# Grouped-query attention, 32 heads: the turns of the step three back are issued ahead of the new scores in each step, instead of behind them

## The chip, the core and the metric

One core of a Trainium2 chip. The metric is the device time of one execution, in microseconds; lower is better. The program has five instruction streams: TensorE (PE; its weight loads are shown as PEld), VectorE (DVE), ScalarE (ACT), GpSimd (POOL) and the DMA queues that SyncE and GpSimd feed. They meet only at semaphores.

## The reference

A chain of four cross-attention layers on `x` (2, 512, 512) against a context (2, 1024, 512). The change lies in the second, layer L1:

```python
H, NH, KVH, HD = 512, 32, 8, 16        # 32 heads of 16, 8 key/value heads
q = hidden_state @ Wq + bq             # 512 rows
k = encoder_hidden_state @ Wk + bk     # 1024 rows
v = encoder_hidden_state @ Wv + bv
q = q.reshape(b, l, KVH, GROUPS, HD).transpose(0, 2, 3, 1, 4)
...
scores = jnp.einsum('bkgld,bksd->bkgls', q, k) * scale
scores = scores + encoder_attention_mask[:, :, None, :, :]
attn = jax.nn.softmax(scores, axis=-1)
out = jnp.einsum('bkgls,bksd->bkgld', attn, v)
out = out.transpose(0, 3, 1, 2, 4).reshape(b, l, H)
out = out @ Wo + bo
x = out + hidden_state                 # then a layer norm
```

The other layers (one-head attention, 16 heads of 128 twice with an MLP, 16 heads of 32 with an MLP) are the same in both kernels.

## The kernel before

The program runs a list of stages for batch 0 and then again for batch 1. The stage of layer L1 is the function `grouped`. Its main loop has 128 steps and a tail of 16 (`STEPS`, `TAIL`): four groups c of eight heads (one quarter of the 512 columns), and in a group 8 heads x 4 blocks of 128 query rows. A step q is one head and one block: 128 rows against 1024 keys. It goes through the engines as a pipeline:

- S(q), TensorE, line 767 (777 after): the scores, two products of 48 x 128 by 48 x 512 into two PSUM banks. There are two pairs of banks, used in turn. S(q) waits for `s_free`: D(q-2) has read this pair.
- D(q), VectorE, line 904: adds the mask, negates, takes the row's minimum, and writes the result to `units` in SBUF (a ring of U = 5). It signals `s_free`.
- E(q), ScalarE, line 850: the exponential in place, with the row sum. It is issued one step later (`LAG_E` = 1) and signals `e_done`.
- T(k), TensorE, line 779 (757 after): eight transposes of 128 x 128 that turn the probabilities, in two halves h of four, each into a bank of its own. They are issued in step q = k + 3 (`LAG_T` = 3). Each half waits for `e_done` of step k and for `t_free[h]`: the copy of the half of T(k-1) has been made. There is a single bank for each half.
- The copies out of these banks, in the same step: the first half by ScalarE (line 858), the second by VectorE (line 915, C(k) below), right behind D(q) on VectorE. Each signals its `t_free`.
- PV, TensorE, line 791: for each head two groups of four products with the values, issued in steps 8 and 9 behind the head's first (`LAG_PV` = 8), so two steps in four have one.

One ring bank serves the rest, behind PV in the steps of `ring_in`: the query projection of the next group (three products in each of steps 16 to 19 of a group), the spread of the reciprocals (step 4), the fold of the parts (step 7: line 813 on TensorE, then lines 928 and 930 on VectorE with line 875 of ScalarE between them), and the output projection (three products in each of steps 10 to 13, added by VectorE, line 936).

Each engine takes its instructions in the order in which its function issues them: `pe_`, `act_` and `dve_` all loop over the same q. In `act_` a step is E(q-1), then the copy of the first half of T(q-3). In `dve_` a step is D(q), then C(q-3):

```python
dve.wait_ge(s_full, n + 1)
dve.tensor_tensor_reduce(units[...], ps[...], mask[...], ...).then_inc(s_free, 1)
...
k = q - LAG_T
dve.wait_ge(t_full[1], n + 1)
dve.tensor_copy(turned[...], ps[:, T_BANK + 1, :]...).then_inc(t_free[1], 1)
```

Of the kernel before, what the change touches and what calls it, by code (L numbers as in the profile page):

```python
# [30 lines left out]
P = 128  # L31
# [77 lines left out]
def build(nc, t, out):  # L109
# [3 lines left out]
    def sem(name):  # L113

        if name not in sems:
            sems[name] = ctx.enter_context(nc.semaphore(name))
        return sems[name]

    with ctx:
        uid = [0]  # L120

        def sb(stack, name, shape, dt=F32):
            uid[0] += 1
            return stack.enter_context(nc.sbuf_tensor(f"{name}_{uid[0]}", shape, dt))
# [29 lines left out]
        ps = ctx.enter_context(nc.psum_tensor("ps", [P, 8, 512], F32))  # L154
        S_BANK, T_BANK, R_BANK = 0, 4, 6


        ident = sb(ctx, "ident", [P, P])
# [376 lines left out]
        def grouped():  # L535
# [4 lines left out]
            U = 5  # L540
            STEPS = C * 32
            TAIL = 16
            LAG_E, LAG_T, LAG_PV = 1, 3, 8
# [5 lines left out]
            units = sb(own, tag + "_units", [P, U, NK])  # L549
# [30 lines left out]
            e_done = sem(tag + "_exp_done")  # L580
            t_full = [sem(f"{tag}_turn_full{i}") for i in range(2)]
            t_free = [sem(f"{tag}_turn_free{i}") for i in range(2)]
# [8 lines left out]
            def ring_of(x):  # L591
                return ps[:, x[2], :] if x[0] == "o" and x[1] == C - 1 else ring
# [14 lines left out]
            def upto(eng, s, n):  # L607
                if n > 0:
                    eng.wait_ge(s, n)

            def ring_turn(pe, b, x):
                if x[0] == "o" and x[1] == C - 1:
                    pe.wait_ge(s_free, (b + 1) * STEPS)
                elif ring_at[x]:
                    y, n = ring_jobs[ring_at[x] - 1], b * 2 * C
                    s_, n = {"q": (kq_done, b * KQ + 2), "rzb": (rzb_done, n), "fold": (a32_done, n),
                             "o": (o_added, n * LT)}[y[0]]
                    pe.wait_ge(s_, n + 1 + (y[1] * LT + y[2] if y[0] == "o" else y[1]))
# [106 lines left out]
            def pe_kv(pe, b, n, w):  # L725
                pe.wait_ge(split["kv"], b * 2 + n + 1)
                for h in range(2):
                    for k in range(KC):
                        i = mm3(pe, ps[:, 2 * n + h, :], w[:, k, :], CT[:, k, h * 512:(h + 1) * 512],
                                k == 0, k == KC - 1)  # L730
                    i.then_inc(pre_full, 1)

            def pe_(pe, b):
                pe_kv(pe, b, 0, wk)
                pe.wait_ge(split["q"], b * C + 1)
                ring_turn(pe, b, ("q", 0))
                pe_q(pe, b, 0, range(KC))
                pe_kv(pe, b, 1, wv)
                for h in range(2):
                    pe.wait_ge(v_done, b * 4 + h + 1)  # L740
                    for q in range(4):
                        i = pe.transpose(ps[:, T_BANK + h, q * P:(q + 1) * P],
                                         vt[:, (4 * h + q) * P:(4 * h + q + 1) * P], ident[:, :])
                    i.then_inc(pre_full, 1)
                pe.wait_ge(kq_done, b * KQ + 2)
                pe.wait_ge(v_done, b * 4 + 4)
                pe.wait_ge(made, b + 1)
                for q in range(STEPS + TAIL):
                    c = q // 32
                    if q < STEPS:  # L750
                        n, i_, u = b * STEPS + q, q % 4, q % 32 // 4
                        if q == 0:
                            pe.wait_ge(first_ready, (b + 1) * 2 * 6 * 16)
                        elif q == 4:
                            pe.wait_ge(qs_ready[0], (b * 15 + 3) * 6 * 16)
                        elif q % 32 == 0:
                            pe.wait_ge(qs_ready[0], (b * 15 + 3 + 4 * c) * 6 * 16)
                        elif q % 32 == 16:
                            pe.wait_ge(qs_ready[1], (b * C + c + 1) * 4 * 6 * 16)
                        if q == 16:  # L760
                            pe.wait_ge(ks_ready[0], (b + 1) * 6 * 16)
                        elif q == 32:
                            pe.wait_ge(ks_ready[1], (b + 1) * 6 * 6 * 16)
                        upto(pe, s_free, n - 1)
                        for h in range(2):
                            p0 = 64 * h
                            i = pe.matmul(ps[:, 2 * (q % 2) + h, :],  # L767
                                          qs[p0:p0 + 3 * DH, u, i_ * P:(i_ + 1) * P],
                                          ks[p0:p0 + 3 * DH, 2 * c + u // 4, :],
                                          start=True, stop=True, skip_group_check=True)  # L770
                        i.then_inc(s_full, 1)
                    k = q - LAG_T
                    if 0 <= k < STEPS:
                        n = b * STEPS + k
                        pe.wait_ge(e_done, n + 1)
                        for h in range(2):
                            upto(pe, t_free[h], n)
                            for v in range(4):
                                i = pe.transpose(ps[:, T_BANK + h, v * P:(v + 1) * P],  # L779
                                                 units[:, k % U, (4 * h + v) * P:(4 * h + v + 1) * P], ident[:, :])  # L780
                            i.then_inc(t_full[h], 1)
                    hd, h = divmod(q - LAG_PV, 4)
                    if 0 <= hd < C * HEADS and h < 2:
                        pair = b * (C * 4) + hd // 2
                        pe.wait_ge(t_free[h], b * STEPS + 4 * hd + 4)
                        if hd % 2 == 0 and h == 0:
                            upto(pe, o_free, pair)
                        for j in range(4):
                            v, kv = 4 * h + j, hd // 4
                            lhs = vd[:, v, kv, 16:48] if hd % 2 == 0 else vd[:, v, kv, 0:32]  # L790
                            i = pe.matmul(ps[32 * j:32 * j + 32, O_BANK, :], lhs, turned[:, hd % 2, v, :],
                                          start=hd % 2 == 0 and h == 0, stop=hd % 2 == 1 and h == 1,
                                          skip_group_check=True)
                        i.then_inc(pv_done, 1)
                    if q % 32 in (16, 17, 18) and c + 1 < C:
                        if q % 32 == 16:
                            pe.wait_ge(split["q"], b * C + c + 2)
                            ring_turn(pe, b, ("q", c + 1))
                        pe_q(pe, b, c + 1, (q % 32 - 16,))
                    for x in ring_in[q]:  # L800
                        if x[0] == "q":
                            pe_q(pe, b, c, (3,))
                            continue
                        g = b * C + x[1]
                        ring_turn(pe, b, x)
                        if x[0] == "rzb":
                            pe.wait_ge(rzx_done, g + 1)
                            for lt in range(LT):
                                i = pe.transpose(ring[:, lt * P:(lt + 1) * P], rzx[:, lt, :], ident[:, :])
                        elif x[0] == "fold":  # L810
                            pe.wait_ge(o_free, (g + 1) * 4)
                            for p_ in range(4):
                                i = pe.matmul(ring[32 * p_:32 * p_ + 32, :], fold[:, :], parts[:, p_, :],
                                              start=True, stop=True, skip_group_check=True)
                        else:
                            lt = x[2]
                            if lt == 0:
                                pe.wait_ge(att_done, b * 2 * C + x[1] + 1)
                                pe.wait_ge(split["o"], g + 1)
                            i = mm3(pe, ring_of(x), att[:, lt * P:(lt + 1) * P], wo[:, :], True, True)  # L820
                        i.then_inc(ring_full, 1)
                barrier(pe, done, b)
# [1420 lines left out]
```

## Time and profile before

| | |
|---|---|
| median of three runs | 4287.23 us (4285.82 to 4290.34) |
| the profiled execution | 4284.18 us, its span 4282.4 us |
| instructions in the span | 55226 |
| PE busy | 3984.2 us, 93% of the span |
| DVE busy | 2556.9 us, 60% |
| ACT busy | 1868.4 us, 44% |
| granted TensorE clock, mean | 0.974 |

The rows further down come from this one profiled execution, which lies 3.05 us under the median. Times are microseconds from the start of the span. The loop of the grouped stage runs from about 153 to 451 us for batch 0 and from about 2291 to 2590 us for batch 1. The two levels of the granted clock are 1.00 (2.4 GHz) and 0.50 (1.2 GHz).

### The profile page before, as it was taken

To read this page: it belongs to the slowest core of one execution; us is meant where nothing else is said; L and a number is where in the kernel's file an instruction comes from. 1 tells how busy PE (TensorE), PEld (TensorE's weight loads), DVE (VectorE), ACT (ScalarE), POOL (GpSimd) and SP (SyncE) were. 2 spreads that over 40 slices of the span, in tenths; PEclk is the share of its full clock that TensorE was granted. 3 is DMA by queue.
4 is the path that set the end of the run, shared out by engine and by line. 5 is a ranking of instruction groups with operands and counts; after the bars stand their busy time and mean duration, and the time that the engine had idled before them with its cause. 6 is when DMAs were issued, how large, how long until landed. Compare 5 with 4: busy or idle time off the path is not lost. (4 is left out here: it accounts for less than half of the span.)

```text
span 4282.4 us, 55226 instructions
## 1 busy us (share of the span) xinstructions
PE 3984.2 (93%) x21018; PEld 2967.9 (69%) x21018; DVE 2556.9 (60%) x4134; ACT 1868.4 (44%) x3294; POOL 1189.7 (28%) x1318
## 2 busy tenths in 40 slices
PE   8899799998999989999988998999989999899988
PEld 6555588887888867543775556888878888775437
DVE  3588656556565665455636886565565656645555
ACT  3588434344443431455135884344343434314551
POOL 0642213223231323121306422132232313232213
PEclk9999899999999999999999999999999999999999
DMA  2310101011010113221403101010110101132212
GB/s 70 74 31 18 55 23 45 23 45 40 28 40 28 40 40 90 51 52 30 130 30 77 28 18 55 23 45 29 39 40 28 45 23 40 45 89 50 50 35 87
DMA packets 167573, 195.62 MB, mean 46 GB/s; under 512 B 18627, under 2 KB 123272, under 8 KB 167310
## 3 DMA queue, kind: packets, MB, share of 16 engines
q1 hardware_dynamic: 142734, 151.15, 11.6%
q0 software_dynamic: 24576, 40.94, 5.0%
q8 instruction: 169, 2.77, 0.3%
q14 instruction: 94, 0.77, 0.1%
HBM read 149.02 MB, written 2.10 MB: 35 GB/s over the span
## 5 line engine op out<-in xcount | busy, mean ns | idle before, releaser
L1337 DVE TENSOR_TENSOR w_pt_lo<-ps,w_pt_hi 128x512 fp32r<-128x512 f32 x512 | 334.7, 685 | 158.7 <-ACT w_pt_hi L1268 158.6
L1113 POOL CAST w_wo_hi<-w_raw 128x1024 fp32r<-128x1024 f32 x32 | 33.2, 1037 | 1329.7 <-PE ps L149 1324.0
L1268 ACT ACTIVATE w_pt_hi<-ps 128x512 fp32r<-128x512 f32 x512 | 281.3, 595 | 203.7 <-PE ps L1205 203.6
L904 DVE CUSTOM_DVE_ANT_0 g_units<-ps,g_mask 128x1024 f32<-128x1024 f32 x256 | 311.2, 1217 | 81.2 <-PE ps L767 81.2
L1754 ACT ACTIVATE h_pt<-ps,zero_col 128x512 f32<-128x512 f32 x384 | 257.1, 686 | 234.3 <-PE ps L1710 232.8
L1803 DVE TENSOR_REDUCE h_mxs<-ps 128x1 f32<-128x512 f32 x384 | 243.7, 684 | 162.5 <-PE ps L1699 160.8
L1320 DVE TENSOR_REDUCE w_mx<-ps 128x1 f32<-128x1024 f32 x256 | 312.0, 1219 | 33.8 <-PE ps L149 33.3
L1205 PE MATMUL ps<-ident,w_p 128*128 128x128 f32 x2048 | 279.1, 275 | 39.6 <-DVE w_pt_lo L1337 39.6
L779 PE MATMUL ps<-ident,g_units 128*128 128x128 f32 x2048 | 292.2, 284 | 19.7 <-ACT g_turned L858 17.4
L850 ACT ACTIVATE g_units<-g_units,g_nmx 128x1024 f32<-128x1024 f32 x256 | 294.6, 1151 | 18.8 <-DVE g_nmx L904 15.8
L1205 PEld LDWEIGHTS ps<-ident,w_p 128*128 128x128 f32 x2048 | 235.2, 140 | 96.2 <-DVE w_pt_lo L1337 67.1
L147 PE MATMUL ps<-w_wv_hi,CT_hi 128*128 128x256 f32 x1024 | 289.1, 282 | 8.6 <-DVE w_v_lo L1331 8.6
L779 PEld LDWEIGHTS ps<-ident,g_units 128*128 128x128 f32 x2048 | 222.0, 143 | 100.1 <-issue 64.3
L149 PE MATMUL ps<-w_wv_hi,CT_lo 128*128 128x256 f32 x1024 | 288.5, 282 | 0.0
L148 PE MATMUL ps<-w_wv_lo,CT_hi 128*128 128x256 f32 x1024 | 288.4, 282 | 0.0
L1261 ACT ACTIVATE w_p<-ps,w_nm 128x1024 f32<-128x1024 f32 x256 | 281.1, 1098 | 0.0
L1259 ACT ACTIVATE w_ex<-w_xl,w_nm 128x1 f32<-128x1 f32 x256 | 75.5, 295 | 420.7 <-DVE w_nm L1326 420.7
L1296 DVE SCALAR_TENSOR_TENSOR w_k_lo<-ps,cols,w_k_hi 128x512 fp32r<-128x512 f32 x128 | 95.7, 750 | 212.0 <-ACT w_k_hi L1243 212.0
L147 PE MATMUL ps<-w_pt_hi,w_v_hi 128*128 128x512 f32 x512 | 217.3, 424 | 0.0
L147 PE MATMUL ps<-w_k_hi,w_q_hi 128*128 128x512 f32 x512 | 210.3, 411 | 7.1 <-ACT w_p L1261 7.1
L1681 PE MATMUL ps<-h_pt,h_vd 128*64 128x512 f32 x768 | 210.5, 626 | 6.6 <-ACT h_parts L1762 6.0
L147 PEld LDWEIGHTS ps<-w_wv_hi,CT_hi 128*128 128x128 f32 x1024 | 195.9, 191 | 14.7 <-DVE w_v_lo L1331 9.4
(362 smaller groups left out, 10209.2 us busy)
## 6 DMA issues: line engine op xcount, KB each, us to landing
w_raw<-in_L_xattn_wk SPq DMA_DIRECT2D x32, 512.0 KB, 3.4
w_raw<-in_L_xattn_wq SPq DMA_DIRECT2D x32, 512.0 KB, 3.5
w_raw<-in_L_xattn_wv SPq DMA_DIRECT2D x32, 512.0 KB, 3.8
w_raw<-in_L_xattn_wo SPq DMA_DIRECT2D x32, 512.0 KB, 3.6
mlp_raw<-in_L_xattn_w_fc SPq DMA_DIRECT2D x64, 256.0 KB, 3.2
mlp_raw<-in_L_xattn_mlp_w SPq DMA_DIRECT2D x64, 256.0 KB, 3.2
h_ks<-h_k_hi POOLq DMA_DIRECT2D x64, 192.0 KB, 3.0
g_qs<-g_q_hi POOLq DMA_DIRECT2D x256, 32.0 KB, 1.9
```

What stands on the lines that cost most here:

```text
L147: pe.matmul(o, a[0], b[0], start=start, stop=False, skip_group_check=True)
L148: pe.matmul(o, a[0], b[1], start=False, stop=False, skip_group_check=True)
L149: return pe.matmul(o, a[1], b[0], start=False, stop=stop, skip_group_check=True)
L779: i = pe.transpose(ps[:, T_BANK + h, v * P:(v + 1) * P], units[:, k % U, (4 * h + v) * P:(4 * h + v + 1) * P], ident[:, :])
L850: act.activation(units[:, k % U, :], units[:, k % U, :], ACT.Exp, bias=nmx[:, k % U:k % U + 1], scale=-1.0, accum_out=z[:, k // 32 % 2, lt ...
L904: dve.tensor_tensor_reduce(units[:, q % U, :].rearrange("p (h w) -> p h w", h=2), ps[:, 2 * (q % 2):2 * (q % 2) + 2, :], mask[:, q % 4, :] ...
L1205: i = pe.transpose(ps[:, T_BANK + tn % 2, lt * P:(lt + 1) * P], prob[:, u, lt, v * P:(v + 1) * P], ident[:, :])
L1261: act.activation(prob[:, u, lt, :].rearrange("p (h w) -> p h w", h=2), ps[:, S_BANK + 2 * (sn % 2):S_BANK + 2 * (sn % 2) + 2, :], ACT.Exp, ...
L1268: act.activation(pt.h[:, x[2] % 4, :], ps[:, T_BANK + tn % 2, :], ACT.Copy).then_inc(t_hi, 1)
L1320: dve.tensor_reduce(mx[:, u, lt:lt + 1], ps[:, S_BANK + 2 * (sn % 2):S_BANK + 2 * (sn % 2) + 2, :], AX.XY, ALU.max).then_inc(max_own, 1)
L1337: dve.tensor_tensor(pt.l[:, x[2] % 4, :], ps[:, T_BANK + tn % 2, :], as_f32(pt.h[:, x[2] % 4, :]), ALU.subtract).then_inc(t_free, 1)
L1754: act.activation(pt[:, j, :], ps[:, T_BANK_ + (m * KT + j) % 2, :], ACT.Exp, bias=zero_col[:, :], scale=SCALE).then_inc(e_done, 1)
```

## The change

In `pe_` the block that issues T(q-3) moves from behind S(q) to ahead of it. Nothing else changes: no operation is added or removed, the semaphores and their counts are the same, and the streams of the other engines are the same.

```diff
                 for q in range(STEPS + TAIL):
                     c = q // 32
+                    k = q - LAG_T
+                    if 0 <= k < STEPS:
+                        n = b * STEPS + k
+                        pe.wait_ge(e_done, n + 1)
+                        for h in range(2):
+                            upto(pe, t_free[h], n)
+                            for v in range(4):
+                                i = pe.transpose(ps[:, T_BANK + h, v * P:(v + 1) * P],
+                                                 units[:, k % U, (4 * h + v) * P:(4 * h + v + 1) * P], ident[:, :])
+                            i.then_inc(t_full[h], 1)
                     if q < STEPS:
                         n, i_, u = b * STEPS + q, q % 4, q % 32 // 4
...
                         i.then_inc(s_full, 1)
-                    k = q - LAG_T
-                    if 0 <= k < STEPS:
-                        n = b * STEPS + k
-                        pe.wait_ge(e_done, n + 1)
-                        for h in range(2):
-                            upto(pe, t_free[h], n)
-                            for v in range(4):
-                                i = pe.transpose(ps[:, T_BANK + h, v * P:(v + 1) * P],
-                                                 units[:, k % U, (4 * h + v) * P:(4 * h + v + 1) * P], ident[:, :])
-                            i.then_inc(t_full[h], 1)
                     hd, h = divmod(q - LAG_PV, 4)
```

TensorE's instructions in the plain steps 9 and 10 of the first batch, before (L767 is S, L779 T, L791 PV; `g_scores_free` is `s_free`, `g_exp_done` is `e_done`, `g_turn_free1` is `t_free[1]`):

```order
L767 MATMUL ps<-g_ks,g_qs 128x512 [waits g_scores_free]
L767 MATMUL ps<-g_ks,g_qs 128x512
L779 MATMUL ps<-ident,g_units 128x128 [waits g_turn_free0,g_exp_done]
L779 MATMUL ps<-ident,g_units 128x128 x3
L779 MATMUL ps<-ident,g_units 128x128 [waits g_turn_free1]
L779 MATMUL ps<-ident,g_units 128x128 x3
L791 MATMUL ps<-g_turned,g_vd 32x512 [waits g_turn_free1]
L791 MATMUL ps<-g_turned,g_vd 32x512 x3
L767 MATMUL ps<-g_ks,g_qs 128x512 [waits g_scores_free]
```

The same place after (L777 is S, L757 T):

```order
L777 MATMUL ps<-g_ks,g_qs 128x512 [waits g_scores_free]
L777 MATMUL ps<-g_ks,g_qs 128x512
L791 MATMUL ps<-g_turned,g_vd 32x512 [waits g_turn_free1]
L791 MATMUL ps<-g_turned,g_vd 32x512 x3
L757 MATMUL ps<-ident,g_units 128x128 [waits g_turn_free0,g_exp_done]
L757 MATMUL ps<-ident,g_units 128x128 x3
L757 MATMUL ps<-ident,g_units 128x128 [waits g_turn_free1]
L757 MATMUL ps<-ident,g_units 128x128 x3
L777 MATMUL ps<-g_ks,g_qs 128x512 [waits g_scores_free]
```

PV now follows S at once, and between PV and the next S stand the eight turns with their two waits.

The second place is the step of the fold (step 7 of the second head group), on TensorE before; L813 is the fold:

```order
L779 MATMUL ps<-ident,g_units 128x128 [waits g_turn_free1]
L779 MATMUL ps<-ident,g_units 128x128 x3
L813 MATMUL ps<-g_parts,g_fold 32x512 [waits g_o_free,rzb_done]
L813 MATMUL ps<-g_parts,g_fold 32x512 x3
L767 MATMUL ps<-g_ks,g_qs 128x512 [waits g_scores_free]
```

and after:

```order
L777 MATMUL ps<-g_ks,g_qs 128x512 [waits g_scores_free]
L777 MATMUL ps<-g_ks,g_qs 128x512
L813 MATMUL ps<-g_parts,g_fold 32x512 [waits g_o_free,rzb_done]
L813 MATMUL ps<-g_parts,g_fold 32x512 x3
L757 MATMUL ps<-ident,g_units 128x128 [waits g_turn_free0,g_exp_done]
L757 MATMUL ps<-ident,g_units 128x128 x3
L757 MATMUL ps<-ident,g_units 128x128 [waits g_turn_free1]
```

The fold now stands right behind the scores of its step. VectorE's stream, which is the same in both kernels, has at this place the copy, the two operations that follow the fold, and the next pass over scores:

```order
L904 ISA g_units,g_nmx<-ps,g_mask 128x1024 [waits g_turn_full1,g_scores_full]
L904 ISA g_nmx 128x1
L915 COPY g_turned<-ps 128x4x128 [waits g_turn_full1,g_pv_done]
L928 TENSOR_TENSOR g_a_61<-ps,g_rzb 128x512 [waits rzb_done,g_ring_full]
L930 SCALAR_TENSOR_TENSOR g_att_lo<-g_a_61,cols,g_att_hi 128x512 [waits att_hi]
L904 ISA g_units,g_nmx<-ps,g_mask 128x1024 [waits g_turn_full1,g_scores_full]
```

Nothing moved there; what moved is when TensorE hands it the scores of the last row.

## Rows read from the trace of the kernel before

**Rows 1.** The page: span, and busy time by engine.

```profile
span 4282.4 us, 55226 instructions
...
PE 3984.2 (93%) x21018; PEld 2967.9 (69%) x21018; DVE 2556.9 (60%) x4134; ACT 1868.4 (44%) x3294; POOL 1189.7 (28%) x1318
```

**Rows 2.** Windows: the first batch's loop, S(0) to past S(127); clock after the engines.

```profile
core 0: us, PE busy (x) PEld busy (x) DVE busy (x) ACT busy (x) POOL busy (x), PEclk, DMA share, GB/s
153.30:443.40 290.10, 276.02 (x1844) 154.53 (x1844) 240.97 (x405) 232.34 (x403) 128.53 (x245) 0.98 0.17 31
```

**Rows 3.** Waits in the first batch's loop: total, times, longest.

```profile
DVE g_units L904 <- PE ps L767: 40.7, 53, 3.2
...
PE ps L779 <- ACT g_turned L858: 7.8, 24, 0.5
...
PEld ps L779 <- DVE g_turned L915: 3.3, 10, 0.4
```

**Rows 4.** Order of time, TensorE only, plain steps: start, duration, instruction.

```profile
431.74 0.50 PE L767 MATMUL ps<-g_ks,g_qs 48*128 48x512 f32 x2
432.17 1.09 PE L779 MATMUL ps<-ident,g_units 128*128 128x128 f32 x8
433.19 0.49 PE L767 MATMUL ps<-g_ks,g_qs 48*128 48x512 f32 x2
...
436.50 1.06 PE L791 MATMUL ps<-g_turned,g_vd 128*32 128x512 f32 x8
437.50 0.51 PE L767 MATMUL ps<-g_ks,g_qs 48*128 48x512 f32 x2
...
439.95 0.50 PE L767 MATMUL ps<-g_ks,g_qs 48*128 48x512 f32 x2
```

**Rows 5.** Order of time, VectorE in the first of these steps.

```profile
432.28 1.22 DVE L904 CUSTOM_DVE_ANT_0 g_units<-ps,g_mask 128x1024 f32<-128x1024 f32 x1 [0.61 <-PE ps L767]
...
433.43 0.69 DVE L915 COPY g_turned<-ps 128x512 f32<-128x512 f32 x1
```

**Rows 6.** Order of time: a second half that waited for VectorE's copy.

```profile
332.91 1.21 DVE L904 CUSTOM_DVE_ANT_0 g_units<-ps,g_mask 128x1024 f32<-128x1024 f32 x1
...
334.05 0.69 DVE L915 COPY g_turned<-ps 128x512 f32<-128x512 f32 x1
...
334.78 0.42 PEld L779 LDWEIGHTS ps<-ident,g_units 128*128 128x128 f32 x4 [0.29 <-DVE g_turned L915]
335.37 0.18 PEld L767 LDWEIGHTS ps<-g_ks,g_qs 48*128 48x128 f32 x2 [0.17 <-issue]
```

**Rows 7.** Order of time, TensorE: S to S with PV and three projection products.

```profile
339.10 0.50 PE L767 MATMUL ps<-g_ks,g_qs 48*128 48x512 f32 x2
...
342.45 0.50 PE L767 MATMUL ps<-g_ks,g_qs 48*128 48x512 f32 x2
```

**Rows 8.** Order of time, VectorE: the first operation behind the fold, the next pass.

```profile
315.60 0.69 DVE L928 TENSOR_TENSOR g_a<-ps,g_rzb 128x512 f32<-128x512 f32 x1
...
317.75 1.22 DVE L904 CUSTOM_DVE_ANT_0 g_units<-ps,g_mask 128x1024 f32<-128x1024 f32 x1
```

**Rows 9.** Order of time: steps 4 and 5 of batch 0, clock at 0.50.

```profile
162.05 0.80 PE L767 MATMUL ps<-g_ks,g_qs 48*128 48x512 f32 x2 [3.12 <-DMA g_qs<-g_q_lo]
...
162.77 1.97 PE L779 MATMUL ps<-ident,g_units 128*128 128x128 f32 x8
162.88 1.23 DVE L904 CUSTOM_DVE_ANT_0 g_units<-ps,g_mask 128x1024 f32<-128x1024 f32 x1 [3.23 <-PE ps L767]
...
164.67 0.79 PE L767 MATMUL ps<-g_ks,g_qs 48*128 48x512 f32 x2
```

**Rows 10.** Order of time, TensorE: S(127) of batch 0, S(4) and S(127) of batch 1.

```profile
441.40 0.49 PE L767 MATMUL ps<-g_ks,g_qs 48*128 48x512 f32 x2
...
2299.38 0.79 PE L767 MATMUL ps<-g_ks,g_qs 48*128 48x512 f32 x2 [2.92 <-DMA g_qs<-g_q_lo]
...
2580.10 0.49 PE L767 MATMUL ps<-g_ks,g_qs 48*128 48x512 f32 x2
```

**Rows 11.** Windows: a stretch of the next stage, and the loop's first 11.7 us.

```profile
504.00:508.00 4.00, 2.32 (x10) 1.61 (x9) 1.83 (x4) 3.34 (x7) 0.00 (x0) 1.00 0.51 140
...
153.30:165.00 11.70, 6.84 (x28) 4.44 (x28) 6.81 (x12) 6.21 (x11) 11.70 (x25) 0.61 0.49 70
```

## The prediction

> **What bounds the kernel now.** Read the page first for which engine is full, then the windows to find out whether that holds in the stage that the change touches, then the waits, and last the order of time, because only there is it seen who releases whom. The page has TensorE busy for 93% of a span of 4282.4 us [rows 1]. The grouped stage runs twice, once a batch, and its main loop is 128 steps long; over that loop TensorE is busy for 276.0 of 290.1 us at a granted clock of 0.98, VectorE for 241.0 and ScalarE for 232.3 [rows 2]. So TensorE bounds the loop, but VectorE is close behind: per step 290.1 / 128 = 2.27 us, of which VectorE works 1.88. The waits are small on TensorE's side: the turns wait 7.8 us in all for the copies of ScalarE, their weight loads 3.3 us for those of VectorE, while VectorE waits 40.7 us for scores [rows 3]. That last wait is no loss: VectorE is the faster of the two and runs out of scores in the steps in which TensorE also has a weighted sum to do.
>
> In what follows S(q) is the score product of step q, D(q) VectorE's pass over it (line 904), T(k) the eight turns of step k, in two halves, C(k) VectorE's copy of the second half (line 915), and PV the four products of a weighted sum. In the order of time a step without PV takes TensorE 433.19 - 431.74 = 1.45 us, of which S to T is 0.43 and T to the next S 1.02; a step with PV takes 439.95 - 437.50 = 2.45, the PV being 437.50 - 436.50 = 1.00 [rows 4]. Two steps in four have one.
>
> **Why the order matters.** T(q-3)'s second half needs the bank that C(q-4) empties. VectorE does C(q-4) right behind D(q-1), and D(q-1) needs S(q-1). Before, S(q) stands ahead of T(q-3), so while VectorE is busy with D(q-1) and C(q-4) the next scores are already being made, and D(q) follows C(q-4) without a pause. After, S(q) stands behind T(q-3) and so behind its wait. TensorE can't make S(q) until C(q-4) has ended, and VectorE, whose next instruction is D(q), stands still meanwhile. What was a chain over two steps with a score bank in hand becomes a ring through both engines in each step. That S could slip past is excluded by the trace: at 334.78 the second half of a turn starts 0.04 us after the end of the copy that held it, and the scores behind it start at 335.37, although the D of two steps back, all that they wait for, had ended by 332.91 + 1.21 = 334.12; TensorE ran them in order [rows 6].
>
> **The price of the ring, link by link.** From S's start to D's start 432.28 - 431.74 = 0.54 us [rows 4, 5]. D to C 433.43 - 432.28 = 1.15, C itself 0.69 [rows 5]. From the end of C (334.05 + 0.69 = 334.74) to the second half's weight load 0.04; from there to the S behind it 335.37 - 334.78 = 0.59 [rows 6]. The sum is 3.01 us a step. Nothing else of a plain step is longer: TensorE needs 1.45 or 2.45, ScalarE 232.3 / 128 = 1.82 [rows 2]. PV and the first half of T lie beside D and C, at no cost, since 2.45 is under 3.01; were that cover gone, a step would cost its 2.45 and more. ScalarE's exponential and its copy gain slack.
>
> *Steps.* The first four steps of a batch fill the pipe and step 4 waits for a DMA until 162.05 in any case [rows 9]; from there to S(127) are 123 steps, 441.40 - 162.05 = 279.35 us in the first batch and 2580.10 - 2299.38 = 280.72 in the second [rows 9, 10]: 560.1 in both. After: 246 x 3.01 = 740.5.
>
> *Steps in which TensorE is longer than the ring.* A PV step that also holds three products of the next projection or of the output projection takes 342.45 - 339.10 = 3.35 us of TensorE [rows 7], 0.34 over the ring. By the code these are steps 12 and 13 of three head groups and 16 and 17 of three: 12 a batch, 24 x 0.34 = 8.2. The same products in steps without PV (3.35 - 1.00 = 2.35) are covered now.
>
> *The fold,* three times a batch before S(127): behind C, VectorE does two more operations with one of ScalarE between them, 317.75 - 315.60 = 2.15 us to the next D [rows 8]. D of that step to the next: 1.15 + 0.69 + 2.15 = 3.99, 0.98 over the ring, 6 x 0.98 = 5.9. Other extra work of VectorE (one addition, of about line 928's 0.69, or a reciprocal) fits into the 1.17 us in which it waits for S.
>
> *The start at the low clock.* Steps 4 and 5 run at 1.2 GHz in both kernels: S to D 162.88 - 162.05 = 0.83, half of T to S (164.67 - 162.77) / 2 = 0.95 [rows 9], so the ring there is 0.83 + 1.15 + 0.69 + 0.04 + 0.95 = 3.66, 0.65 more: four such steps, 2.6.
>
> Sum without any further loss of clock: 740.5 + 8.2 + 5.9 + 2.6 - 560.1 = **+197 us**. The last steps, without S, change by under 1 us: the same turns and PVs follow each other.
>
> **The clock.** TensorE is now nearly always busy and granted 0.98 [rows 2]. In the new loop it is still 0.56 us ahead of the second half of T in a PV step and 1.56 us in a step without. By the durations of its S and T, 0.50 + 1.09 = 1.59 of 3.01 us [rows 4], a step without PV is busy for 53%, a little more when T's halves stand apart, and two such steps stand together. Rows at such a share go both ways: four microseconds at 2.32 / 4.00 = 58% kept 1.00, while the first 11.7 us of this loop at 6.84 / 11.70 = 58% were granted 0.61 [rows 11]. So part of the steps may run at 1.2 GHz, and I have no row that fixes which part. The bounds: none, +0; all of them, where a step without PV costs the 0.65 above and one with PV 2.62 (164.67 - 162.05) + 2 x 1.00 = 4.62, 1.61 over the ring: 1.13 in the mean, x 246 = +278. PV steps are full at 1.2 GHz, and the loop before, full, was granted 0.98 [rows 2], so the clock should come back each time; hence nearer to none than to all. I take a quarter of the steps: 62 x 1.13 = **+70**. The Trainium skill ("TensorE: Matmul & The Clock Gate", section "A second HAM failure mode: psum-queue depth-cycling") says that brief idling between groups of matmuls, frequent enough, makes the clock oscillate between its two levels; read strictly it speaks for half of the steps or more (+139 and up), and the rows at 58% agree with it only in part.
>
> **Forecast.** 4284.18 (the profiled execution) + 197 + 70 = 4551. That execution is 3.05 us below the median of the three timed runs, 4287.23, so in terms of the median 4554.
>
> **The rivals.**
> *The clock stays at 2.4 GHz.* For it: 58% with 1.00 in one row. Then 4287 + 197 = 4484.
> *The clock is low for more than half of the steps.* For it: once low, a step without PV stays light. 4484 + 139 to 4484 + 278: 4623 to 4762.
> *Nothing changes,* since TensorE does the same work and is the bound (95% busy). This would need C(q-4) to be done when TensorE comes to the second half. In the old order it nearly always is, 3.3 us of such waits in a batch [rows 3]; but there S and D are a step ahead, and the new order takes just that away. 4287.
> *Faster:* the turns come earlier in a step, so the copies and PV have more slack, and TensorE's idle time in the loop goes. All of it is 290.1 - 276.0 = 14.1 us a batch, so 4287 - 28 = 4259. This decides only if the ring is under TensorE's 1.95 us a step; it is 3.01, so two of its links would have to vanish.
> *A partial ring:* if a link overlaps another in a way that the old order never shows, the ring might be 2.5 us: 246 x 2.5 + 17 - 560 = +72, 4359.
>
> **How the numbers follow.** Forecast (ring, part of the steps at the low clock, 4510 to 4640): 0.50. Clock stays (4475 to 4510): 0.33. Clock low for more than that: 0.09. Partial ring: 0.03. Nothing changes: 0.03. Faster: 0.02. The range 4475 to 4640 holds the first two; the clock's share, from none to 56% of the steps, makes its width. A measurement of this kernel tells about 0.2% from no change; slower by over 0.2% is 0.95, same 0.03, faster 0.02.
>
> **What the new profile would show.** Right: S starts 3.0 us apart in plain steps; in each of them VectorE's D idles about 1.2 us for the scores (over 100 us a batch, 40.7 before), and the weight load of the second half waits for C, 0.5 to 1.5 us each (over 80 us, 3.3 before); TensorE's busy share in the loop falls to 75% or so, ScalarE's to 60%; the rest of the program keeps its times. The clock shows in the windows over the loop: about 0.87 for a quarter of the steps, 0.98 or more for the first rival. Wrong: steps of about 2.2 us; C ending before TensorE reaches the turn; or a wait on ScalarE's copy or exponential ahead of the turns in place of that on VectorE's copy.

## The result, and the profile after

| | before | after |
|---|---|---|
| median | 4286.52 us (4283.12 to 4290.34, 4 runs) | 4554.91 us (4548.05 to 4558.12, 4 runs) |
| ratio to before, 95% interval | 1 | 1.0625 [1.061, 1.064] |
| profiled execution, its span | 4284.18, 4282.4 | 4548.05, 4546.2 |
| granted clock, mean | 0.974 | 0.949 |
| loops, S(4) to S(127), both batches | 560.1 us | 831.4 us |

The change makes the kernel 268 us slower; the forecast was 4554.0. The page of the changed kernel answers to [rows 1]: the span, the busy times, the granted clock in 40 slices, and the four costliest groups.

```profile
span 4546.2 us, 55226 instructions
PE 4110.8 (90%) x21018; PEld 3011.0 (66%) x21018; DVE 2571.6 (57%) x4134; ACT 1867.2 (41%) x3294; POOL 1187.5 (26%) x1318
...
PEclk9888889999999999999998888899999999999999
...
L757 PE MATMUL ps<-ident,g_units 128*128 128x128 f32 x2048 | 377.6, 321 | 161.8 <-DVE g_turned L915 144.3
L904 DVE CUSTOM_DVE_ANT_0 g_units<-ps,g_mask 128x1024 f32<-128x1024 f32 x256 | 313.1, 1224 | 356.5 <-PE ps L777 356.5
L757 PEld LDWEIGHTS ps<-ident,g_units 128*128 128x128 f32 x2048 | 264.2, 162 | 360.0 <-DVE g_turned L915 196.2
L850 ACT ACTIVATE g_units<-g_units,g_nmx 128x1024 f32<-128x1024 f32 x256 | 294.0, 1149 | 333.1 <-DVE g_nmx L904 333.1
```

The work is the same, yet TensorE is busy for 127 us more. Most of that is slower instructions: the steps of the two loops that the low clock touches are busy some 101 us longer than steps of the same kind at full clock, and the 8s in the clock's line, in slices 2 to 6 and 22 to 26, show where. The rest is that the turns now stand in two groups apart, which overlap less with their neighbours: a plain step at full clock is busy for 1.71 us, where it was 1.51. The second number behind each bar is the idle time ahead of the group: the turns wait for VectorE's copy (L915), VectorE's D waits 356.5 us for scores, and ScalarE's exponential 333.1 us for D. Three engines wait for each other in turn, which is how a ring looks in a page.

The windows from S(4) to S(127) of either batch, after, answer to [rows 2]; each engine's busy time with its instructions, then the granted clock:

```profile
core 0: us, PE busy (x) PEld busy (x) DVE busy (x) ACT busy (x) POOL busy (x), PEclk, DMA share, GB/s
160.77:576.58 415.81, 338.62 (x1819) 176.44 (x1818) 240.91 (x393) 225.53 (x394) 119.19 (x227) 0.83 0.11 20
2431.38:2846.96 415.58, 335.87 (x1819) 176.49 (x1818) 240.96 (x393) 225.58 (x394) 118.62 (x226) 0.84 0.11 20
```

The same 123 steps took 279.35 and 280.72 us before [rows 9, 10]. The two loops grow by 831.4 - 560.1 = 271.3 us, which is more than the 4546.2 - 4282.4 = 263.8 by which the whole profiled execution grows; the rest of the program is 7.5 us shorter.

The waits of the first batch's loop, after (total, times, longest), answer to [rows 3]:

```profile
engine line waited for: us in total, times, longest us
DVE g_units L904 <- PE ps L777: 172.7, 120, 3.2
ACT g_units L850 <- DVE g_nmx L904: 161.4, 114, 2.2
...
PEld ps L757 <- DVE g_turned L915: 94.8, 95, 1.6
PE ps L757 <- DVE g_turned L915: 69.3, 95, 1.3
```

The order of time of the changed kernel, a step with PV, then one without, then one in which the clock has fallen (start, duration; in brackets the idle time before and what ended it):

```profile
246.98 0.50 PE L777 MATMUL ps<-g_ks,g_qs 48*128 48x512 f32 x2
...
247.41 1.06 PE L791 MATMUL ps<-g_turned,g_vd 128*32 128x512 f32 x8
...
249.42 0.66 PE L757 MATMUL ps<-ident,g_units 128*128 128x128 f32 x4 [0.35 <-DVE g_turned L915]
...
250.00 0.50 PE L777 MATMUL ps<-g_ks,g_qs 48*128 48x512 f32 x2
...
250.55 1.22 DVE L904 CUSTOM_DVE_ANT_0 g_units<-ps,g_mask 128x1024 f32<-128x1024 f32 x1 [1.18 <-PE ps L777]
...
250.66 0.63 PE L757 MATMUL ps<-ident,g_units 128*128 128x128 f32 x4 [0.16 <-ACT g_turned L858]
...
251.70 0.69 DVE L915 COPY g_turned<-ps 128x512 f32<-128x512 f32 x1
...
252.44 0.66 PE L757 MATMUL ps<-ident,g_units 128*128 128x128 f32 x4 [1.15 <-DVE g_turned L915]
...
253.02 0.63 PE L777 MATMUL ps<-g_ks,g_qs 48*128 48x512 f32 x2
...
253.68 1.08 PE L757 MATMUL ps<-ident,g_units 128*128 128x128 f32 x4
```

The ring can be walked in these rows. S starts at 250.00, D at 250.55, C at 251.70 and ends at 252.39, the second half starts at 252.44, the next S at 253.02: 0.55 + 1.15 + 0.69 + 0.05 + 0.58 = 3.02 us. The step ahead of it has a PV and takes 250.00 - 246.98 = 3.02 as well: PV lies inside the ring and only shortens TensorE's wait, from 1.15 to 0.35 us. At 253.02 the clock falls (S takes 0.63, four turns 1.08 instead of 0.63), and the next S comes 3.61 us later.

### The profile page after: what moved, and what is told of

It reads as the page before. It is cut to its first block and busy times, and to the rows that moved or that the text cites. A ratio compares the mean times of both kernels' runs of the same rounds, so it can differ in the third digit from the quotient of the medians.

```text
span 4546.2 us, 55226 instructions
## 1 busy us (share of the span) xinstructions
PE 4110.8 (90%) x21018; PEld 3011.0 (66%) x21018; DVE 2571.6 (57%) x4134; ACT 1867.2 (41%) x3294; POOL 1187.5 (26%) x1318
## 5 line engine op out<-in xcount | busy, mean ns | idle before, releaser
L757 PE MATMUL ps<-ident,g_units 128*128 128x128 f32 x2048 | 377.6, 321 | 161.8 <-DVE g_turned L915 144.3
L904 DVE CUSTOM_DVE_ANT_0 g_units<-ps,g_mask 128x1024 f32<-128x1024 f32 x256 | 313.1, 1224 | 356.5 <-PE ps L777 356.5
L757 PEld LDWEIGHTS ps<-ident,g_units 128*128 128x128 f32 x2048 | 264.2, 162 | 360.0 <-DVE g_turned L915 196.2
L850 ACT ACTIVATE g_units<-g_units,g_nmx 128x1024 f32<-128x1024 f32 x256 | 294.0, 1149 | 333.1 <-DVE g_nmx L904 333.1
L147 PE MATMUL ps<-CT_hi,w_wk_hi 128*128 128x512 f32 x512 | 201.9, 394 | 3.9 <-DVEq L232 3.9
```

The source lines that it names most:

```text
L147: pe.matmul(o, a[0], b[0], start=start, stop=False, skip_group_check=True)
L757: i = pe.transpose(ps[:, T_BANK + h, v * P:(v + 1) * P], units[:, k % U, (4 * h + v) * P:(4 * h + v + 1) * P], ident[:, :])
L850: act.activation(units[:, k % U, :], units[:, k % U, :], ACT.Exp, bias=nmx[:, k % U:k % U + 1], scale=-1.0, accum_out=z[:, k // 32 % 2, lt ...
L904: dve.tensor_tensor_reduce(units[:, q % U, :].rearrange("p (h w) -> p h w", h=2), ps[:, 2 * (q % 2):2 * (q % 2) + 2, :], mask[:, q % 4, :] ...
```

## The experiments

Two theories stood against each other from the start. The ring: what costs is that the second half's bank is emptied by a copy which VectorE does behind D, so that with T ahead of S each step pays the whole circle. The rival: turns ahead of the scores delay these by the turns' own length, 1.02 us in a step, whichever copy frees the bank. And for what goes beyond the ring, 79 us as worked out below: a lower clock, or more ring.

Ratios are to the kernel before, run on the same chip (its medians there were 4282.11, 4284.27 and 4283.69 us), with 95% intervals; they are worked out over all runs and need not be the quotient of the two medians. "Loops" is S(4) to S(127) of batch 0 and of batch 1.

| edit | median us (range) | ratio | loops us |
|---|---|---|---|
| only the first half ahead of S | 4328.91 (4328.38 to 4335.7) | 1.0115 [1.0098, 1.0132] | 304.7 + 304.7 |
| only the second half ahead of S | 4573.56 (4570.35 to 4576.87) | 1.0681 [1.0665, 1.0697] | 426.9 + 426.6 |
| after, second half ahead of the first | 4717.68 (4712.31 to 4725.26) | 1.1019 [1.1002, 1.1035] | 492.7 + 497.3 |
| after, filler products in the wait | 4539.63 (4534.61 to 4556.27) | 1.0609 [1.0587, 1.063] | 402.4 + 404.2 |
| the same in fewer steps | 4497.8 (4493.42 to 4499.71) | 1.0504 [1.0488, 1.0521] | 387.3 + 384.6 |
| after, VectorE's copy first | 4387.81 (4384.19 to 4402.1) | 1.0255 [1.0233, 1.0277] | 325.3 + 335.0 |
| before, VectorE's copy first | 4381.59 (4380.15 to 4384.05) | 1.0232 [1.0216, 1.0247] | 324.7 + 331.3 |
| before, ScalarE's copy first | 4289.5 (4281.98 to 4294.64) | 1.0013 [1.0004, 1.0023] | 285.7 + 283.7 |
| after, both copies first | 4274.52 (4269.74 to 4280.33) | 0.9984 [0.9974, 0.9993] | 277.4 + 276.3 |
| before, both copies first | 4289.9 (4285.04 to 4294.0) | 1.0012 [1.0003, 1.0021] | 282.3 + 283.4 |

### One half at a time

The block of the turns is cut in two; one half stays ahead of S, the other goes back behind it.

```diff
-                        for h in range(2):      # ahead of S
+                        for h in (0,):
...
+                        for h in (1,):          # the same block again, behind S
```

> Only the first half of the turns (the four that wait for ScalarE's copy) stands ahead of the scores; the second half (the four that wait for VectorE's copy) is back behind them. Ring theory: the scores no longer wait for VectorE's copy of the step before, so the ring through scores, VectorE's pass, its copy and the second half is gone. What is left is a ring through ScalarE over two steps: pass to exponential 1.27 us, exponential 1.33, ScalarE's copy 0.60, first half 0.50, scores to pass 0.54, 4.24 us or 2.12 a step, under TensorE's mean of 2.27 with the projections. Expected 4287, between 4280 and 4330; clock over the loop 0.97 or more. Rival (turns ahead of the scores delay them by their own length, wait or no wait): half of the turns, half of the loss, about 4287 + 135 = 4420.

The other way round, `(1,)` ahead and `(0,)` behind:

> Only the second half of the turns stands ahead of the scores, the first half behind them. Ring theory: the ring is whole (scores to pass 0.54, pass 1.15, copy 0.69, 0.04, second half 0.59: 3.02 us a step), so the loss is that of the change, 4500 to 4590 with the clock's share, most likely 4550. Rival (turns ahead delay by their own length): half of the loss, about 4420.

The first half alone costs 1.2%, the second alone more than the whole change. (Its ring is a little longer: at full clock a step takes 3.08 us, which over 246 steps is 15 of the 22 us by which its loops exceed those of the changed kernel.) The turns moved ahead of S are four in both cases; only the copy that frees their bank differs. That rules the rival of the turns' own length out, and puts the loss on VectorE's copy. The order of time of the first kernel shows what its 1.2% is (L860 is the exponential there, L868 ScalarE's copy, L925 VectorE's):

```profile
442.18 0.42 PEld L757 LDWEIGHTS ps<-ident,g_units 128*128 128x128 f32 x4 [0.73 <-ACT g_units L860]
442.21 0.63 PE L757 MATMUL ps<-ident,g_units 128*128 128x128 f32 x4 [0.52 <-ACT g_turned L868]
442.77 0.50 PE L777 MATMUL ps<-g_ks,g_qs 48*128 48x512 f32 x2
```

A second, weaker ring goes through ScalarE: the first half needs the copy that ScalarE makes behind its exponential, which needs D of the step before. It spans two steps. Four steps, two of them with PV, took 9.41 us (S at 442.77 and again at 452.18); before, such a four took 439.95 - 431.74 = 8.21 [rows 4]. Of the 1.20 us between them, 0.3 is no wait at all: the two steps with PV take 2.59 and 2.60 where they took 2.45, and TensorE is never idle in them, but the turns stand in two groups of four with the PV between, 0.58 us each to what follows, where eight together took 1.02. The other 0.9 lies in the two steps without PV. In the first of them the turns wait 0.38 us for VectorE's copy (L925), in the second 0.52 for ScalarE's, as in the rows above. I had 4287 with a range of 4280 to 4330. I had foreseen the ring through ScalarE, but at 2.12 us a step, too short to bind, and had not thought of the split turns.

### The halves in the other order

```diff
-                        for h in range(2):
+                        for h in (1, 0):
```

> As the changed kernel, all turns ahead of the scores, but the second half is issued before the first. Ring theory: between VectorE's copy and the scores stand eight turns now, not four, so the ring is longer by the four of the first half, 0.43 us: 3.45 a step, 246 x 0.43 = 106 over the changed kernel, and more of it at the low clock: 4620 to 4720, most likely 4665. Rival (turns ahead delay the scores by their own length): the same turns are ahead, so no change, 4555.

Now both halves stand between the end of C and the next S. The order of time, in the first batch:

```profile
502.33 1.23 DVE L904 CUSTOM_DVE_ANT_0 g_units<-ps,g_mask 128x1024 f32<-128x1024 f32 x1 [1.68 <-PE ps L777]
...
503.48 0.69 DVE L915 COPY g_turned<-ps 128x512 f32<-128x512 f32 x1
...
504.31 1.06 PE L757 MATMUL ps<-ident,g_units 128*128 128x128 f32 x8 [1.03 <-DVE g_turned L915]
...
505.30 0.49 PE L777 MATMUL ps<-g_ks,g_qs 48*128 48x512 f32 x2
```

C ends at 504.17, S comes 1.13 later; the step is 505.30 - 501.79 = 3.51 us against 3.02. S to D and D to C are as they were (0.54 and 1.15), and the ring grew behind C: the turns take 0.99 us to the next S instead of 0.58, and start 0.14 behind C instead of 0.05. 4717.68 is 163 us over the changed kernel: 246 x 0.49 = 121 for the ring and, by difference, some 42 for the clock, which over its first loop was granted 0.77 against 0.83. I had 4665: the clock's part was too small.

### Is the rest the clock?

TensorE gets useless work in its idle time: the step's pair of score products three times more, into the pair of banks that S is about to overwrite, between the two halves of T. The waits for the score operands and for this pair of banks move ahead of the turns with it. As long as the filler ends before C does, it changes nothing in the ring.

```diff
+                            if h == 1 and q < STEPS and not (q >= LAG_PV and (q - LAG_PV) % 4 < 2):
+                                for _ in range(FILL):            # FILL = 3
+                                    for g in range(2):
+                                        pe.matmul(ps[:, 2 * (q % 2) + g, :], qs[...], ks[...], ...)
                             upto(pe, t_free[h], n)
```

> The changed kernel with extra work on TensorE that nobody needs: in the steps without a weighted sum the step's score products are made three times more, between the two halves of the turns, into the bank that the real ones overwrite (1.29 us, in which TensorE otherwise waits for VectorE's copy). The score operands and the bank are waited for ahead of the turns. Ring theory with the clock as a term of its own: the ring stays 3.02 us, the work is hidden, and the clock over the loop goes from 0.83 to 0.97 or more, so the steps at the low clock (77.6 us in the trace of the changed kernel) come back: 4555 - 78 = 4477, between 4465 and 4500, faster with more work. Rival (the long steps are long for another reason than the clock): 4555 or more.

That missed: 4539.63 is 40 us above the end of the range. The turns of step q are issued behind the PV of step q - 1, so in half of the chosen steps the filler stood where TensorE waits 0.35 us and not 1.15 (L775 is the filler, L781 the turns, L788 S):

```profile
227.26 0.66 PE L781 MATMUL ps<-ident,g_units 128*128 128x128 f32 x4
227.84 0.97 PE L775 MATMUL ps<-g_ks,g_qs 48*128 48x512 f32 x6
228.74 0.66 PE L781 MATMUL ps<-ident,g_units 128*128 128x128 f32 x4
```

From filler to second half there is no wait left: the filler itself set the step's end. In these places the steps took 3.49 us instead of 3.02, and 4.25 where a projection stood beside the PV. The clock was up (0.97 and 0.96 over the loops, 20 of the 246 steps below full clock), but the filler ate the gain. So again, with the filler only where the step ahead has neither PV nor another product:

```diff
+                            if h == 1 and q < STEPS and (q - LAG_PV) % 4 in (0, 3) and q % 32 not in (11, 12, 19, 20, 7, 8):
```

> The filler of the run before this one, put where TensorE really has the room: between the halves of the turns only where the step before holds no weighted sum, no projection and no fold (there the second half waited 1.15 us for VectorE's copy, and three extra score products take 0.90). Before, half of the filler stood behind a weighted sum, where the wait is 0.35 us, and lengthened the ring by itself. Clock theory: the ring stays 3.02 us in all steps, the clock over the loop is 0.95 or more, and of the 78 us of steps at the low clock at least 60 come back: 4477 to 4500. Rival (the long steps are long for another reason): 4550 or more.

```profile
230.65 0.50 PE L788 MATMUL ps<-g_ks,g_qs 48*128 48x512 f32 x2
231.31 0.63 PE L781 MATMUL ps<-ident,g_units 128*128 128x128 f32 x4 [0.16 <-ACT g_turned L869]
231.87 0.96 PE L775 MATMUL ps<-g_ks,g_qs 48*128 48x512 f32 x6
233.08 0.66 PE L781 MATMUL ps<-ident,g_units 128*128 128x128 f32 x4 [0.25 <-DVE g_turned L926]
233.67 0.50 PE L788 MATMUL ps<-g_ks,g_qs 48*128 48x512 f32 x2
```

The ring is still 233.67 - 230.65 = 3.02 us, TensorE does more work than in the changed kernel, and the median is 57 us lower. The loops lost 831.4 - 771.9 = 59.5 us, at a granted clock of 0.94 and 0.96 in place of 0.83 and 0.84. So most of what goes beyond the ring, 59.5 of 79 us, is the clock, and the clock falls because of the ring's idle time. The trace accounts for the other 19.5 us too: 29 of the 246 steps are still below full clock in this kernel, and they are 20.2 us longer than the ring.

### Breaking the ring

In `dve_` the copy of the second half goes ahead of D, so that it no longer waits for the D of the step:

```diff
                 for q in range(STEPS + TAIL):
                     c = q // 32
+                    k = q - LAG_T
+                    if 0 <= k < STEPS:
...
+                        dve.tensor_copy(turned[...], ps[:, T_BANK + 1, :]...).then_inc(t_free[1], 1)
                     if q < STEPS:
...
                                                  nmx[:, q % U:q % U + 1]).then_inc(s_free, 1)
-                    k = q - LAG_T
...
-                        dve.tensor_copy(turned[...], ps[:, T_BANK + 1, :]...).then_inc(t_free[1], 1)
```

> The changed kernel with VectorE's two operations of a step in the other order: the copy of the turns of three steps back first, then the pass over the new scores. Ring theory: VectorE's copy no longer stands behind the pass, so the ring through the pass and the copy (3.02 us) is gone although all turns still stand ahead of the scores. What is left is the ring through ScalarE over two steps: pass 1.27, exponential 1.33, ScalarE's copy 0.60, eight turns 1.05, VectorE's copy 0.60: 4.9 us, 2.45 a step. Expected 4340, between 4300 and 4400. Rival (turns ahead delay the scores by their own length whatever VectorE does): 4555.

167 us come back, 48 fewer than I expected. The step is as forecast, 2.46 us in the median against 2.45; but 29 steps are below full clock, and they are some 32 us longer than that. The waits of its first loop (L906 is VectorE's copy there, L912 D) show what is left:

```profile
PEld ps L757 <- ACT g_units L850: 100.3, 91, 2.0
...
DVE g_turned L906 <- PE ps L757: 78.8, 105, 2.6
...
PE ps L757 <- ACT g_turned L858: 49.6, 60, 1.7
```

The wait for VectorE's copy is gone, and the turns wait for ScalarE instead, for the exponential and for the copy behind it. On ScalarE the same move is to be made (`act_`: the copy of T(q-3) ahead of E(q-1)); with both:

> As the kernel with VectorE's copy first, and ScalarE in the same order too: its copy of the first half first, then the exponential of the step before. Ring theory: both copies follow their turns at once, no ring is longer than TensorE's own 1.45 and 2.45 us, so TensorE is the bound as before and its idle time of 14 us a batch goes at least in part: 4265, between 4250 and 4290, at the order of TensorE that lost 6%. Rival (turns ahead of the scores are bad in themselves): over 4400.

4274.52 us, 280 us under the changed kernel and 0.16% under the kernel before. That also shows that the ring through ScalarE was what the run before it had left. A window of the length of its first loop, from half a microsecond ahead of S(4):

```profile
160.87:438.20 277.33, 268.32 (x1815) 154.32 (x1815) 234.15 (x392) 219.30 (x390) 119.92 (x228) 0.99 0.16 31
```

TensorE's order is that of the changed kernel, to the instruction. Nothing of the 268 us was in that order itself; all of it was in how it met the orders of VectorE and ScalarE.

### The same copies in the kernel before

To know whether the studied change or the copies make that kernel fast, the copies were moved in the kernel before too.

> The kernel before (scores ahead of the turns) with ScalarE's copy ahead of its exponential. If ScalarE's copy behind the exponential is what the turns still wait for (7.8 us a batch, and some of the exponential's 10.2), 4265 to 4282; if the exponential then comes too late instead, 4287 or more. This is the comparison for the kernel with both copies first: it shows whether the order of TensorE matters once the copies are first.

> The kernel before (scores ahead of the turns) with VectorE's copy ahead of its pass. With the scores first, the copy has to wait for turns that are issued behind the scores, and the pass stands behind it: the pass ends about 3.4 us after the start of its scores (eight turns 1.45, copy 0.70, pass 1.23), and the scores of two steps on wait for it where two steps without a weighted sum take TensorE 2.9 us. Ring theory: 0.5 us in each such pair, 62 of them: 4310, between 4295 and 4340. If instead VectorE's order costs nothing here, 4284.

> The kernel before with both copies first: it differs from the fastest kernel so far (both copies first, turns ahead of the scores, 4275) only by the change that is studied. Ring theory: the order on TensorE and the order on VectorE have to match; here they don't, and the same 0.5 us a pair as with VectorE's copy first alone is lost: 4310, between 4290 and 4340, so with the copies first the change makes the kernel faster by some 35. Rival (turns ahead of the scores cost something in themselves): at or below 4275.

ScalarE's copy first alone changes nothing much (1.0013); the gain of up to 20 us that I held possible did not come. VectorE's copy first alone costs 98 us, where I had looked for 26: D comes later, so the exponential comes later, ScalarE's copy stands behind that, and the turns wait for both (165 to 470 us, in a loop that runs from 163 to 488):

```profile
PEld ps L779 <- ACT g_units L850: 56.9, 47, 1.6
...
PE ps L779 <- ACT g_turned L858: 43.9, 50, 1.3
```

With both copies first the 98 us are back down to 6 (4289.9), 20 below the 4310 that I expected. There the studied change, turns ahead of the scores, is worth 4289.9 - 4274.52 = 15 us of gain, where I had expected 35. Its place is seen in the waits of the first loop in the kernel before with both copies first:

```profile
PE ps L767 <- DVE g_nmx L912: 11.0, 22, 0.6
```

The scores wait 11.0 us for D, which VectorE now does later, and their weight loads 24.9 us. With the turns ahead of them the scores' own wait is not among TensorE's any more and that of the weight loads is 4.3 us; the loops are 282.3 - 277.4 = 4.9 and 283.4 - 276.3 = 7.1 us shorter. Whether the other 3 of the 15 us belong to the change is not settled; the medians of the kernel before beside the two differ by 0.6 us.

## Why the prediction was right

**The ring** is what the forecast says, link by link: 3.02 measured, 3.01 worked out; D's waits 172.7 us in a batch (over 100 forecast), the second half's weight loads 94.8 us in 95 waits (over 80). The experiments on its links in the changed kernel (either half alone, the halves' order, VectorE's copy first) moved the time the way that the ring says every time.

**Steps longer than the ring.** A step of PV with three more products takes 3.19 us, not 3.35: the 0.34 of the forecast was 0.17, 4.1 us instead of 8.2. [Rows 7] hold no wait either, but other seams: there S came 0.33 us behind the start of the last of the three products and the eight turns took 1.02 to what follows, while now the turns come 0.24 behind it and take 0.96 to the next S. The fold's step takes 3.89 us where nothing disturbs it (three of six), 0.87 over the ring against 0.98. The other three follow steps at the low clock and take 4.32, 3.77 and 3.74. In the first two of these line 930 also takes twice its time, which is told under the hardware below. All six are 5.4 us over the ring, forecast 5.9; without line 930's longer times it would be some 3.9, so this term was mis-sized too, and came out near by luck.

**The sum without the clock.** 246 x 3.02 + 4.1 + 5.4 = 752.4 us for the two loops, 192.3 over before; the forecast's first part was 197, with 2.6 for the low clock at the start in it.

**The clock** costs the rest, 831.4 - 752.4 = 79.0 us, against +70 forecast. Two sizes in that term were wrong, and they cancel. By the durations of TensorE's instructions, 96 of the 246 steps hold one made at the low level, 39% and not a quarter; such a step costs 79.0 / 96 = 0.82 us and not 1.13, because many are low only in part and a PV step that is low throughout takes 4.49 us, not 4.62. The other 150 steps are 3.01 to 3.05 long but for the 18 with projections and the six of the fold. A plain step at the low level takes 3.77, where 3.66 was worked out; from the second half of the turns to S it is 1.05 there (163.49 to 164.54) and not 0.95:

```profile
160.77 0.80 PE L777 MATMUL ps<-g_ks,g_qs 48*128 48x512 f32 x2
164.54 0.79 PE L777 MATMUL ps<-g_ks,g_qs 48*128 48x512 f32 x2
```

The clock over the loops was 0.83 and 0.84 where the forecast said about 0.87. That share was a choice, and a row that fixes it did not exist in the trace of before: the 70 came out near 79 by luck in part. TensorE's busy share was 81%, not 75%, for the same reason: slow instructions count as busy. (Without their 101 us it is 574 of 752 us, 76%.) The rule of the Trainium skill ("TensorE: Matmul & The Clock Gate", section "A second HAM failure mode: psum-queue depth-cycling") is borne out as to kind: with brief idling in each step the clock went back and forth between the levels, down at 253.02 and up again by 260.64 in the first loop. The page names no share of the time; the half of the steps or more was my own reading, and did not come.

**Outside the loops** under 1 us was forecast and 7.5 us went: 1.3 ahead of the first loop, 3.2 between the two (1854.80 us after, 1857.98 before) and 3.0 behind the second (1699.3 and 1702.3), in stages whose instructions are the same. It is 0.2% of the time, as much as executions of the kernel before differ among themselves (4283.12 to 4290.34). Nor does it go with the loops: over the twelve profiled kernels of this document the time outside them lies between 3714.8 and 3726.4 us, in no order of the loops' length (3722.3 before, 3714.8 after, 3723.5 with the halves swapped, the slowest).

**The hit on the microsecond** is luck. Against the forecast of 4551 for the profiled execution the ring's part was 5 us too high, the clock's 9 too low and the rest 7.5 too high, which makes up the 3 us to the 4548 measured; and that execution lies 6.9 us under its median, not 3.05.

**The rivals.** That the clock stays would have been 4484; the filler in the right steps, with the clock nearly up, gives 4497.8. "Nothing changes" and "faster" fell with the waits for VectorE's copy, 1.15 us in a step without PV and 0.35 in one with it. For "faster" the forecast named a condition, that two links of the ring vanish. VectorE's copy first takes out two, S to D and D to C, and was still 2.5% slower than before (4387.81), because the forecast saw only slack on ScalarE and no second ring through it. With ScalarE's copy first as well it came true: 4259 forecast, 4274.52 measured.

## What to carry to other kernels

When a producer is moved ahead of another on one engine, walk one step across all engines and ask of each wait behind which instruction its releaser stands; if the releaser stands behind work that needs what the producer now delays, the step costs the full circle. Let the other engines empty banks in the order in which they are filled: turns first was 6% slower with the copies last, and 0.2% faster with the copies first on both engines. How much a mismatch costs is another matter: scores first with both copies first don't match either, and cost 6 us (4289.9), while with VectorE's copy alone first they cost 98. Before blaming an engine, add the idle time that the ring gives TensorE to the bill, for it can bring the clock down too (79 us of 268 here).

## What was unexpected in the hardware

**The clock.** It fell to 1.2 GHz in a loop in which no wait of TensorE's turns for VectorE's copy is longer than 1.3 us (1.6 for their weight loads) and in which the window has TensorE busy for 81%. Products that nobody needs, put into that idle time, made the kernel 57 us faster and left 29 steps below full clock instead of 96.

**VectorE beside GpSimd.** Line 930, the last operation of the fold on VectorE, takes 0.75 us in four of the six folds of the loops, and twice as long in the two in which GpSimd subtracts beside it for more than 0.9 us (1.54 and 1.52). The changed kernel's order of time, the first fold and the third:

```profile
284.83 1.29 POOL L675 TENSOR_TENSOR g_wq_lo<-g_raw_q,g_wq_hi 128x512 fp32r<-128x512 f32 x1 [0.16 <-issue]
285.12 1.54 DVE L930 SCALAR_TENSOR_TENSOR g_att_lo<-g_a,cols,g_att_hi 128x512 fp32r<-128x512 f32 x1 [0.79 <-ACT g_att_hi L875]
...
289.05 0.50 PE L777 MATMUL ps<-g_ks,g_qs 48*128 48x512 f32 x2
...
499.42 0.75 DVE L930 SCALAR_TENSOR_TENSOR g_att_lo<-g_a,cols,g_att_hi 128x512 fp32r<-128x512 f32 x1 [0.79 <-ACT g_att_hi L875]
...
502.56 0.50 PE L777 MATMUL ps<-g_ks,g_qs 48*128 48x512 f32 x2
```

The S ahead of these stand at 284.73 and 498.67: steps of 4.32 and 3.89 us. In the fold of 1.52 us S came late, by the low clock, and the longer operation showed less: 3.77.

Line 930 looks blocked rather than slowed. It ends at 285.12 + 1.54 = 286.66, which is 0.54 us behind the end of GpSimd's subtraction (284.83 + 1.29 = 286.12). The fold in the tail of the loop, outside the 123 steps, shows the same before and after: there line 930 starts 0.57 us into a longer subtraction (2.34 us), takes 2.32 us and ends 0.55 behind it (455.99 before, 593.06 after). With the halves swapped it starts 0.89 us into that subtraction, takes 2.00 and again ends 0.55 behind it. In that kernel's six folds of the loops, where no subtraction runs beside line 930, it takes 0.75 each time. GpSimd's other operation, a scaling (line 671), does not hold it up so: beside it the line took 0.75 us at 317.08 in the kernel before, where the scaling started just behind it, and 0.75 too with only the first half ahead of S (it is line 940 there, at 252.51), where the scaling had started 0.82 us earlier. So the slower loop only shifted what meets what. The Trainium skill ("Advanced Engine Details and Errata", section "VectorE Performance Modes") says that VectorE's second port into SBUF is shared with GpSimd, so that GpSimd's instructions and those which VectorE runs in a two-port mode block each other. The rows agree with the blocking; no row shows in which mode line 930 ran, and no run was made to take it apart.
